# A four-layer convolution kernel on one core: the mixture-of-experts layer on pairs of images with its gates applied to the input, and the deformable convolution gathered image by image

## The reference

```python
# layer 0: 2x2 patches as tokens (d = 32*2*2 = 128), 8 experts, hidden 256, two experts per token
gate = top-2 of softmax(xp @ router_w), renormalised, 0 for the other six experts
for e in range(8):
    val, g = split(xp @ w1[e]); out += gate[:, e] * ((val * silu(g)) @ w2[e])
# layer 1: deformable 3x3 convolution
om = conv3x3(x);  py, px = base + offsets;  mask = sigmoid(m)
sampled = sum over 4 corners of take(x, corner) * weight * mask   # (32 channels, 9 taps, 32, 32)
y = relu(batchnorm(einsum('bckhw,ock->bohw', sampled, w) + b))
```

## Time and profile before

| | |
|---|---|
| median of 3 runs | 1914.44 us (1912.62 to 1920.05) |
| profiled execution, first to last instruction | 2385.4 us |
| TensorE busy in it | 1477.8 us (62%), mean granted clock 0.782 |
| GpSimd busy | 1200.2 us (50%), of it gathers 1147.6 us |
| VectorE busy | 902.8 us (38%) |
| ScalarE busy | 513.5 us (22%) |

### The profile page before, as it was taken

How to read it: one execution, slowest core, us unless ns; L and a number is a source line. 1 busy time by engine, 2 the same in 40 slices (tenths; PEclk the granted TensorE clock), 3 DMA queues, 4 the chain that set the end, 5 groups by cost and what they waited for, 6 DMA issues and landing times.

```text
span 2385.4 us, 17778 instructions
## 1 busy us (share of the span) xinstructions
PE 1477.8 (62%) x5782; PEld 846.0 (35%) x5782; DVE 902.8 (38%) x1416; ACT 513.5 (22%) x823; POOL 1200.2 (50%) x1393
## 2 busy tenths in 40 slices
PE   6973323465257966774578985674339684138988
PEld 5842222353133433542244443542114231013433
DVE  3532322234242332575332333576313227441235
ACT  2220000112022223112322322112302221023343
POOL 7126675556744644565654654465664546740000
PEclk9976555677578988886678998786669886568999
DMA  4021111112121111112131111112131111111000
GB/s 169 1 56 43 41 51 39 39 34 80 52 65 35 41 29 35 38 38 76 49 74 32 41 37 33 34 47 66 51 80 32 37 32 43 53 32 44 1 0 9
DMA packets 66784, 106.71 MB, mean 45 GB/s; under 512 B 20480, under 2 KB 43904, under 8 KB 66304
## 3 DMA queue, kind: packets, MB, share of 16 engines
q0 software_dynamic: 36864, 75.57, 11.8%
q1 hardware_dynamic: 29248, 26.81, 4.0%
q10 hardware_dynamic: 576, 3.15, 0.3%
HBM read 83.16 MB, written 13.89 MB: 41 GB/s over the span
## 4 chain that ended last, share of the span: by engine, by line
PE 35%; another core or an unknown queue 28%; issue 14%; DVE 9%; ACT 5%; POOL 3%; DMA 1%; DVEq 0%; SPq 0%; ACTq 0%; POOLq 0%
PE bank L1326 9%; PE bank L1311 8%; PE bank L1226 4%; POOL gt L635 3%; PE bank L1357 3%; PE bank L1236 2%; DVE gt L1038 2%; DVE rb L1117 2%; PE bank L1331 2%; PE bank L1266 2%; PE bank L1344 1%; PE bank L1288 1%; PE bank L1385 1%; DVE gt L1039 1%
## 5 line engine op out<-in xcount | busy, mean ns | idle before, releaser
L635 POOL DMA_INDIRECT gt<-corner_table,idx x1152 | 1147.6, 996 | 920.0 <-DVE sm L1044 490.9
L1226 PE MATMUL bank<-xp,w_sb 128*128 128x256 f32 x1024 | 310.4, 452 | 119.1 <-issue 50.9
L1326 PE MATMUL bank<-yg,wts 128*128 128x512 f32 x512 | 257.3, 647 | 46.9 <-ACT tg L758 38.1
L1226 PEld LDWEIGHTS bank<-xp,w_sb 128*128 128x128 f32 x1024 | 221.5, 229 | 179.1 <-issue 66.2
L1311 PE MATMUL bank<-u,wk 128*128 128x512 f32 x512 | 240.9, 620 | 9.0 <-DMA u<-sqb 9.0
L941 DVE SCALAR_TENSOR_TENSOR he<-he,bank 128x512 f32<-128x512 f32 x128 | 87.7, 685 | 399.2 <-ACT he L692 194.1
L1236 PE MATMUL bank<-w_sb,he 128*128 128x128 f32 x1024 | 159.5, 301 | 115.5 <-issue 101.8
L1357 PE MATMUL bank<-xp,musq 128*128 128x512 f32 x212 | 131.0, 765 | 145.5 <-issue 82.4
L1236 PEld LDWEIGHTS bank<-w_sb,he 128*128 128x128 f32 x1024 | 154.8, 216 | 129.8 <-issue 120.6
L1288 PE MATMUL bank<-cst,sm 128*128 128x128 f32 x384 | 82.5, 330 | 189.2 <-DVE sm L1044 84.5
L1038 DVE TENSOR_TENSOR gt<-gt,cw 128x1152 f32<-128x1152 f32 x128 | 173.2, 1353 | 52.9 <-DMA gt<-corner_table,idx 35.4
(11 more groups left out here) (185 smaller groups left out, 1258.2 us busy)
## 6 DMA issues: line engine op xcount, KB each, us to landing
gt<-corner_table,idx POOLq DMA_INDIRECT x1152
corner_table<-tb SPq DMA_DIRECT2D x45, 256.0 KB, 5.6
u<-sqb SPq DMA_DIRECT2D x64, 128.0 KB
w_sb<-w ACTq DMA_DIRECT2D x2, 1024.0 KB, 9.2
out<-X SPq DMA_DIRECT2D x8, 256.0 KB
X<-x SPq DMA_DIRECT2D x1, 1536.0 KB, 18.8
wts<-weights SPq DMA_DIRECT2D x1, 1446.0 KB, 15.3
w_sb<-w ACTq DMA_DIRECT2D x2, 512.0 KB, 12.1
```

Source lines behind the costliest of these rows:

```text
L635: pool.indirect_dma_start(gt[:, g, k].rearrange("p a c -> p (a c)"), None, table, bass.IndirectOffsetOnAxis(ap=idx[:, j, g * KK + k:g * KK ...
L1226: op = mm(psum[b][:, h * TOK:(h + 1) * TOK], w1_sb[:, e, first + h], xp[:, g], start=True, stop=True)
L1326: op = mm(psum[B2.bank(name)][:, :], w_glu[:, k, col + d * P:col + (d + 1) * P], yg[:, c % 2, k], start=k == 0, stop=k == NB2 - 1)
```

## The change

**Layer 0.** A unit is now one half of the hidden units of one expert for a pair of images, so all products have 512 columns; there are again 32 units (2 pairs x 8 experts x 2 halves). The gates are transposed by TensorE once per step (`l0_gates`), and VectorE spreads them to `shares`. For every expert and pair one product with a constant broadcasts its gate over the 128 partitions into bank 0 (`l0_share`), and VectorE multiplies the patches by it into `xg`. The value half is computed from `xg`, the gate half from `xp`. The outputs of all 16 units of a pair accumulate in bank 2, and ScalarE copies them out once per pair. Bank 0 now holds gate halves and shares in turn. The new constants `token` and `expert` are 0/1 masks.

**Layer 1.** Place t is now block j = t % 8 of image g = t // 8. After each four places `dcn(m)` does half an image: three products of 512 columns into the 32 partitions of that image, then ReLU and the add to `X` on these 32 partitions, eight times per step instead of twice.

```diff
-NU = GI * NE
+NU = 2 * NE * 2
+NJ = HALF // P
-A_PLACES = [(0, 2, 6), (2, 17, 9), (17, 22.5, NU + 2 - 15), (22.5, 23.6, 2), (25.2, 27.8, 3 + TQ - 2)]
+A_PLACES = [(0, 2, 7), (2, 17, 9), (17, 22.5, NU + 2 - 15), (22.5, 23.6, 2), (25.2, 27.8, 3 + TQ - 2)]
-        if t and t % GI == 0:
-            parts.append((t, "dcn", t // GI - 1))
+        if t and t % NJ == 0:
+            parts.append((t, "dcn", t // NJ - 1))
 ScalarE
+                if u == NU // 2 + 1:
+                    l0_result(s, 0)
+            def l0_result(s, q):
+                B0.filled(act, s, ("out", q))
+                act.activation(oT[q], psum[2][:, :], ACT.Copy).then_inc(free[2], 1)
+            def dcn(s, m):
+                image = slice(m // 2 * C, (m // 2 + 1) * C)
+                B1.filled(act, s, ("dcn", m))
+                act.wait_ge(S["x1_added"], FROM + s * 2 * GI + m)
+                act.activation(r1[image, :], psum[4][image, :], ACT.Relu, bias=bi1[image, :], scale=sc1[image, :])\
+                   .then_inc(free[4], 1)
 VectorE
-            def l0_acc(s, u):
...
+            def l0_share(s, i):
+                q = i // NE
+                B0.filled(dve, s, ("share", i))
+                tt(xg[:, i % 2], xp[:, 2 * q:2 * q + 2].rearrange("p g n -> p (g n)"), psum[0][:, :], ALU.mult)\
+                    .then_inc(free[0], 1)
+            def l0_unit(s, u):
...
+                B0.filled(dve, s, ("value", u))
+                B0.read(dve, s, ("gate", u))
                 stt(out=he[:, u % 2], in0=he[:, u % 2], scalar=1.0, in1=psum[1][:, :],
                     op0=ALU.add, op1=ALU.mult).then_inc(free[1], 1)
+                if u % 2 and u < NU - 1:
+                    l0_share(s, u // 2 + 1)
+            def dcn(s, m):
+                g, n = divmod(m, 2)
+                image = slice(g * C, (g + 1) * C)
+                B1.read(dve, s, ("dcn", m))
+                xh = X[image, bass.ds(s, 1), n * HALF:(n + 1) * HALF].rearrange("p o n -> p (o n)")
+                tt(xh, xh, r1[image, :], ALU.add).then_inc(S["x1_added"], 1)
 TensorE
+            def l0_gates(s):
+                pe.wait_ge(S["gate_ready"], s + 1)
+                pe.transpose(psum[2][0:8 * NE, 0:P], gate[:, :, :].rearrange("p t e -> p (t e)"), ident)\
+                  .then_inc(full[2], 1)
+                B0.read(pe, s, "turned")
+                l0_share(s, 0)
             def l0_h(s, u):
+                i, h = divmod(u, 2)
+                q, e = divmod(i, NE)
+                B0.vacant(pe, s, ("gate", u))
+                mm(psum[0][:, :], w1_sb[:, e, 2 + h], xp[:, 2 * q:2 * q + 2].rearrange("p g n -> p (g n)"),
+                   start=True, stop=True).then_inc(full[0], 1)
+                B0.read(pe, s, ("share", i))
+                B0.vacant(pe, s, ("value", u))
+                mm(psum[1][:, :], w1_sb[:, e, h], xg[:, i % 2], start=True, stop=True).then_inc(full[1], 1)
+                if h and u < NU - 1:
+                    l0_share(s, i + 1)
             def l0_out(s, u):
+                mm(psum[2][:, :], w2_sb[:, e, h], he[:, u % 2], start=u % (NU // 2) == 0, stop=last)\
+                    .then_inc(full[2] if last else S["he_used"], 1)
             def dcn(s, m):
                 for k in range(3):
-                    for g in range(GI):
-                        op = mm(psum[4][g * C:(g + 1) * C, j % 4 * P:(j % 4 + 1) * P], w_dcn[:, k],
-                                st[:, g, k * P:(k + 1) * P], start=k == 0, stop=k == 2)
+                    op = mm(psum[4][g * C:(g + 1) * C, :], w_dcn[:, k], st[:, k], start=k == 0, stop=k == 2)
```

More of the change, by code:

```diff
@@ L31 @@
 NT = HW // P
+NJ = HALF // P
+GRING = 4
 DM = 256
@@ L158, in plan_b @@
 def plan_b():
[L159 to L163, removed]
+    return [(("dcn", m), 4) for m in range(2 * GI)] + [(("sampled", t), 3) for t in range(NT * GI)]
 def plan_c():
@@ L420, in build @@
         u_in = [sem(f"u_in{g}") for g in range(GI)]
-        gathered = [sem(f"gathered{g}") for g in range(GI)]
+        gathered = [sem(f"gathered{i}") for i in range(GRING)]
         block = ctx.enter_context(nc.Block())
@@ L933, in l0_route @@
                 ch.then(dve.reciprocal(m1[:, :], m1[:, :]))
-                ch.then(stt(out=gate[:, :, :], in0=gate[:, :, :], scalar=0.5, in1=over(m1),
-                            op0=ALU.mult, op1=ALU.mult))
-            def l0_he(s, u):
+                stt(out=gate[:, :, :], in0=gate[:, :, :], scalar=0.5, in1=over(m1),
+                    op0=ALU.mult, op1=ALU.mult).then_inc(S["gate_ready"], 1)
+            def l0_gates(s):
+                B0.filled(dve, s, "turned")
+                op = tt(shares.rearrange("p (t n) -> p t n", t=8),
+                        psum[2][0:8 * NE, 0:P].unsqueeze(1).to_broadcast([8 * NE, 8, P]),
+                        con("token")[0:8 * NE].unsqueeze(2).to_broadcast([8 * NE, 8, P]), ALU.mult)
+                op.then_inc(free[2], 1)
+                l0_share(s, 0)
[5 more added lines that the diff above has]
+            def l0_unit(s, u):
+                if u == NU:
+                    return
                 B0.filled(dve, s, ("value", u))
@@ new lines, in l0_share @@
+            def l0_share(s, i):
+                q, e = divmod(i, NE)
+                B0.vacant(pe, s, ("share", i))
+                mm(psum[0][:, :], con("expert")[0:8 * NE, e:e + 1].to_broadcast([8 * NE, P]),
+                   shares[:, q * HALF:(q + 1) * HALF], start=True, stop=True).then_inc(full[0], 1)
+            def l0_h(s, u):
+                i, h = divmod(u, 2)
+                q, e = divmod(i, NE)
+                B0.vacant(pe, s, ("gate", u))
[6 more added lines that the diff above has]
+                    l0_share(s, i + 1)
@@ L1239, in l0_out @@
-                op.then_inc(full[2], 1)
-            def l0_tail(s):
-                B0.read(pe, s, ("out", NU - 1))
-                for t in range(2):
-                    B0.vacant(pe, s, ("back", t))
-                    for dyx in range(4):
-                        op = pe.transpose(psum[t][:, dyx * P:(dyx + 1) * P],
-                                          acc[:, t, dyx].rearrange("p g c -> p (g c)"),
-                                          ident)
-                    op.then_inc(full[t], 1)
+                if u % (NU // 2) == 0:
+                    B0.vacant(pe, s, ("out", q))
@@ new lines, in l0_out @@
+                last = u % (NU // 2) == NU // 2 - 1
+                mm(psum[2][:, :], w2_sb[:, e, h], he[:, u % 2], start=u % (NU // 2) == 0, stop=last)\
+                    .then_inc(full[2] if last else S["he_used"], 1)
+            def l0_tail(s):
+                for q in range(2):
+                    B0.read(pe, s, ("out", q))
+                for dy in range(PT):
+                    B0.vacant(pe, s, ("back", dy))
+                    for dx in range(PT):
+                        for g in range(GI):
+                            at = (dy * PT + dx) * C
+                            op = mm(psum[dy][g * C:(g + 1) * C, dx * TOK:(dx + 1) * TOK], ident[:, at:at + C],
+                                    oT[g // 2][:, g % 2 * TOK:(g % 2 + 1) * TOK], start=True, stop=True)
+                    op.then_inc(full[dy], 1)
```

180 lines of the change are left out of this document (71 added, 109 removed).

## The result

The changed kernel takes **2013.59 us** (median of 4 runs, 2006.24 to 2017.64) against 1913.53 us for the kernel before (4 runs, 1911.65 to 1920.05): a ratio of 1.0516, interval 1.0484 to 1.0547, so 100 us slower. The forecast was 1963 (range 1895 to 2015), +49 us, so the time measured lies 1.4 us inside the range and outside the forecast's own narrower one, 1940 to 2000.

A forecast was written before the change was run, and what follows sets the result against it. TensorE was taken to bound prologue, end and layer 2 of steps 1 and 2, gathers the other steps. 20 + 0 + 2 x (10 + 3) + 1 + 2 = +49 us, 1914 + 49 = 1963 us, range 1895 to 2015.

The forecast's parts named there:

- rival C: Steps: 24 new waits of `dcn`, at least 4.5 us each, are exposed, 108 us in all; 2044 us, chance 0.08.
- Prologue, +20: Before the first gather: 15 us more TensorE time for units of layer 0 plus 5 for the later start.
- Step 0, 0, step 3, +1, end, +2: Gathers hide step 0's added 15 us; step 3 loses 1 us; the chain after the last place grows 1.8 us.
- Steps 1 and 2, 2 x (10 + 3) = +26: Per step, 10 us in layer 2 (t = 3 to 17), which TensorE paces, and 3 for units behind it.
- slots and idle gaps: Layer 2 of steps 1 and 2: these absorb some of 12.7 us added per step, leaving +10.
- a third: Units at t = 17 to 22.5, steps 1 and 2: a third of their added 8.5 us counts, +3 per step.
- The ledger of 63 us of waits: Ordinary runs: with gathers at 1.25 us, GpSimd waits only some 63 us in the four steps.
- 415 to 546 us: Step lengths claimed for the profiled execution of the kernel before, instead of 360 us.
- Rival A: Slots hide everything in the steps; only prologue and end remain, 1936 us, chance 0.15.
- Rival B: VectorE's order was the limit; relieving it removes two thirds of the 63 us of waits; 1893 us, chance 0.22.
- D: Whole kernel: rival B's gain just pays for the prologue, no change, 1915 us, chance 0.10.
- The profiled execution itself may even become shorter: Profile of the changed kernel: its stalls seem to go with the number of instructions; no size given.

The follow-up runs named there:

- paced: Kernels before, with layer 1's change, layer 0's, or both, each place's nine gathers replaced by eleven memsets: 1888.95, 1924.32, 1944.69 and 2004.97 us.
- paced_after: The changed kernel (both layers) with its gathers replaced by memsets: 2004.97 us, +116.0 against paced_before.
- paced_before: The kernel before with its gathers replaced by memsets, nothing fetched: 1888.95 us, on a chip whose kernel before took 2343.51 us.
- after_again: The changed kernel, unedited, on another chip: 2336.26 us against 2332.81 for the kernel before, ratio 0.9962.

## Why the prediction was right, step by step, and where it was short

**The case.** The forecast case came: TensorE sets the pace in steps 1 and 2, fewer and wider instructions return nothing, and the prologue pays. The sum, 49 us, is half of the 100 (116 paced). That 2013.59 us still lies inside the range is luck: the forecast's own bounds ended at 2000, and the range went on to 2015 for the sake of rival C, which priced the layer 1 half at 108 us where it costs 35. Nearly all of the missing 51 us (67 paced) is in one term.

**Prologue, +20:** measured +22.7 in the recorded pair, +23.8 paced. The unit is 3.20 us where 3.09 was worked out; the share and its two neighbours take 0.95 to 1.05 us, not 0.88. So the unit grew by 0.58 us. With the fixed cost per matmul of the Trainium skill (TensorEngine Tiling (Array Packing), Instruction Overhead), weighed and left aside in the prediction, it would have grown by an estimated 0.25; the trace does not bear that out. The start is +7.9 instead of +5, because the first share and products took twice their time: the share 2.07 us at 32.80 us and 1.12 at 60.53. The first halves of the kernel before were as slow (5.23 us for 12 records in the earlier trace rows, 1.89 for 8 in the earlier trace rows), but hidden behind the routing. From the last `he` to the first gather the kernel after is 2.6 us shorter (44.8 instead of 47.5), which the prediction had as the same. The row of the first share's stretch does not show the slow products, its granted clock is 1.00:

```profile
31.00:35.00 4.00, 2.46 (x3) 0.63 (x3) 1.31 (x2) 0.00 (x0) 3.37 (x20) 1.00 0.00 0
```

**Step 0, 0, step 3, +1, end, +2:** measured paced 0.0, +0.1 and +2.8. The gathers cover the additions there as reckoned; the burst at the low clock in step 0 that the prediction had as an upper bound of 12 us cost nothing.

**Steps 1 and 2, 2 x (10 + 3) = +26: the step that was mis-sized.** Measured 31.4 + 57.9 = **+89** paced. In the recorded pair the steps must have lost some 100 - 23 - 3 = 74 us; the profile of after shows 59.5 us of waits for VectorE in them. By stretches, the two steps together:

- Layer 2, t = 3 to 17: 20 counted, 30 measured. The columns were reckoned well, 12.7 us per step against +10.4 and +12.0 us of busy time. But 2.7 us were taken off for "slots and idle gaps", and the stretch grew by more than its columns, 14.3 and 15.8 us.
- The units behind it: "a third", 3 of 8.5 us per step, was counted, 12.4 measured.
- All other places of the two steps: nothing was counted, 34 us measured. The start of layer 0 had a term of +5 in the prologue and none in the steps, where it comes again, and the other four `dcn` of a step had none either.

The guess of a third and the 2.7 us off rested on rows 8, where TensorE is busy 183 of 231 us at a clock of 0.90, in an execution with stalls in it. Without these it is busy 156 of 160 us at full clock, and what is added there comes out on the other side in full. Over a whole step, 15.0 for shares and 8 x 1.8 = 14 for `dcn` at a clock of 0.92 are some 32 us, against a TensorE busy time of +28 (step 1) and +46 (step 2). Step 2 has more than the columns: ahead of its layer 2 the granted clock is 0.81 instead of 0.95. Beyond that, an engine that is late also adds waits: TensorE's idle time in step 2 grows from 57 to 68 us. The new in-order dependences are visible in it; the waits before the share (L1237) and before the gate product behind it (L1245) in paced_after:

```profile
PE bank L1237 <- DVE cwn L950: 19.5, 4, 7.9
PE bank L1245 <- DVE xg L960: 18.7, 10, 6.8
...
PE bank L1237 <- ACT he L699: 14.8, 8, 2.6
```

They are 53 us over the kernel, part of it in prologue and step 0. How much of the 58 us of step 2 is columns, how much the lower clock and how much these waits, no run separates; the rows of step 2 only show that busy time is 46 of it. That TensorE's added work is the cause is read from the profiles: no variant took the share or the wide `dcn` products alone out of the paced kernel.

**"The ledger of 63 us of waits."** It rested on a pitch of 1.25 us, the usual gather. The mean of the kernel after is 1.325, and 1152 x 0.075 = 86 us: more than the 63. The kernel before waits for nothing in paced_before, and for 0 to 36 us by what can be worked out for the runs. The prediction named a wrong pitch as what would upset its ledger, but thought of faster gathers; they are slower. This did not change the sign: little or nothing was to be won there, and what TensorE adds beyond the gathers' pace is lost.

**The steps' lengths.** "415 to 546 us" are the lengths of the stretches in the earlier trace rows, which do not begin at the steps. From first gather to first gather they take 454, 525 and 527 us, and the last one 469 up to the last gather; nothing in the sum hangs on it.

**Rival A** (all hidden, 1936) fell: TensorE had no room to hide anything in. **Rival B** (VectorE relieved, 1893) fell: there were few or no waits for VectorE to take away; most of the 491 us in the earlier trace rows went with the stalls (0 in paced_before). VectorE's busy time did go down, from 924.1 to 910.9 us paced, 13 against the predicted 12. **Rival C** (waits of `dcn` exposed, 2044) is nearer to the time measured than the forecast (30 against 51 us), but hardly by its mechanism: it priced the layer 1 half at some 108 us, and that half alone costs 35, with 20 us more of TensorE's busy time in step 2 alone. **D** fell.

**"The profiled execution itself may even become shorter":** it did, 2385 to 2004 us, but not for the reason given. `after_again` has the same stalls with the fewer instructions.

**What stays open.** Why the recorded runs of before are undisturbed while its profile and all of its runs on the four chips of the experiments are not. The stalls need the gathers: with memsets in their place the same chip gives 1889 instead of 2344 us. They are seen in copies landing in 5.7 to 6.1 instead of 2.5 us. Which resource is short was not tested, and neither was why on such a chip the changed kernel isn't slower. No variant that keeps the wide units but avoids the losses was tried, such as the changed layer 0 with the gates spread earlier.

## What to carry to other kernels

Before counting on slack, find the part of a step in which the in-order engine is full: a mean of 85% busy was 98% in one part of the step here, and work added there cost its full length, two additions together more than their sum. A cost found at the start of a stage in the prologue comes again in each step, and has to be counted there. Products that write 32 partitions are cheap only while four of them run on different column groups; an order that makes them come one image at a time turns 0.86 us into 2.7. And when a profiled execution is much longer than the runs, take durations of single instructions from it, but no slack, no waits and no busy shares; here a kernel with the disturbed part replaced by a fixed-time one showed them.

## What the runs showed of the hardware that was not expected

- The same kernel takes 1914 us in the recorded runs and 2314 to 2394 us on the four chips of the experiments. With the indirect DMAs replaced by memsets, one of these gives 1889 us instead of 2344.
- An indirect DMA of 128 rows of 512 bytes mostly takes GpSimd 0.94 us and 0.30 until the next, but 1.325 us from start to start in the mean over 1152, waits left out. VectorE is busy for 86% of the time of those above 1.0 us, and for 36% of the time of the others.
- Behind 5.2 us of idle time and a transpose of 0.39, TensorE takes 2.07 us for a product of two records of 512 columns at 32.80 us, and 1.12 for the same one at 60.53, in a stretch whose granted clock reads 1.00 throughout.
